# Expert masks that read exponentials from SBUF and compare them with the exponential of a threshold

## The reference

```python
s1 = einsum('bshd,nd->bshn', q1, K1)            # 8 heads, 32 keys each
s2 = einsum('bshd,nd->bshn', q2, K2)
v1, i1 = top_k(s1, 10);  v2, i2 = top_k(s2, 10)
all_scores = (v1[..., :, None] + v2[..., None, :]).reshape(..., 100)
vals, best = top_k(all_scores, 10)              # the 10 best pairs of a head
scores = softmax(vals)
h = gelu(x . w_down[expert]) * scores
out = einsum('bshk,bshkd->bsd', h, w_up[expert])
```

## Time and profile before

| | |
|---|---|
| median of 3 runs | 1143.75 us (1143.23 to 1144.29) |
| the profiled execution's own time | 1142.8 us |
| its span in the trace | 1141.0 us |
| mean granted TensorE clock | 0.97 (1.00 in the steady rounds) |
| busy: PE, ACT, DVE, POOL | 1015.9, 960.2, 880.9, 824.6 us |
| share of the span | 89%, 84%, 77%, 72% |
| one steady round | 32.42 us |

### The profile page before, as it was taken

How to read it: one execution, slowest core, us unless ns; L and a number is a source line. 1 busy time by engine, 2 the same in 40 slices (tenths; PEclk the granted TensorE clock), 3 DMA queues, 4 the chain that set the end, 5 groups by cost and what they waited for, 6 DMA issues and landing times.

```text
span 1141.0 us, 34446 instructions
## 1 busy us (share of the span) xinstructions
PE 1015.9 (89%) x11656; PEld 769.5 (67%) x11656; DVE 880.9 (77%) x2929; ACT 960.2 (84%) x2252; POOL 824.6 (72%) x871
## 2 busy tenths in 40 slices
PE   3588999999999999999999999999999999999755
PEld 2466777766677777766776777667777776677433
DVE  1427788888888888888888888888888888888763
ACT  1558899999999989999999999999899899998652
POOL 0234777887777777987777778877777788777755
PEclk9899899999999999999999999999999999999875
DMA  5000000000000000000000000000000000000000
GB/s 142 24 13 14 4 14 16 16 14 16 16 12 8 16 16 16 16 14 16 16 4 16 16 16 16 14 16 16 5 15 16 16 16 14 14 13 7 4 3 5
DMA packets 36683, 18.78 MB, mean 16 GB/s; under 512 B 13632, under 2 KB 36256, under 8 KB 36512
## 3 DMA queue, kind: packets, MB, share of 16 engines
q1 hardware_dynamic: 36512, 16.58, 5.4%
HBM read 14.47 MB, written 2.10 MB: 15 GB/s over the span
## 4 chain that ended last, share of the span: by engine, by line
POOL 35%; DVE 21%; issue 14%; ACT 14%; PE 14%; SPq 1%; DMA 1%; POOLq 1%; DVEq 0%; ACTq 0%
POOL wsum L1038 23%; ACT p L649 7%; POOL feat L1022 5%; DVE cand L908 5%; DVE mw L937 4%; DVE best L913 3%; DVE best L903 3%; PE psXT L330 3%; ACT ew L737 3%; PE psXT L414 3%; POOL rstd L976 3%; ACT am L686 2%; PE psF L533 2%; POOL cand L1007 2%; SPq L230 1%
## 5 line engine op out<-in xcount | busy, mean ns | idle before, releaser
L1038 POOL TENSOR_TENSOR wsum<-wsum,mw 128x1024 f32<-128x1024 f32 x192 | 451.8, 2353 | 165.6 <-DVE mw L937 160.0
L937 DVE SCALAR_TENSOR_TENSOR mw<-psF,cut,ew 128x1024 f32<-128x1024 f32 x256 | 326.1, 1281 | 61.9 <-ACT ew L737 58.6
L737 ACT ACTIVATE ew<-psF,lnz 128x1024 f32<-128x1024 f32 x256 | 288.3, 1127 | 14.5 <-PE psF L533 11.3
L649 ACT ACTIVATE p<-psXT,negmax 128x128 f32<-128x128 f32 x512 | 182.2, 387 | 2.6 <-DVE negmax L810 2.5
L533 PE MATMUL psF<-sel,usT 128*128 128x512 f16 x512 | 158.6, 393 | 24.7 <-DVE mw L937 21.8
L330 PE MATMUL psXT<-cT,q 96*128 96x128 f32 x1024 | 141.0, 281 | 22.9 <-ACT p L649 18.5
L330 PEld LDWEIGHTS psXT<-cT,q 96*128 96x128 f32 x1024 | 129.1, 195 | 43.5 <-ACT p L649 35.3
L989 POOL TENSOR_TENSOR p<-p,rrow 128x512 f32<-128x512 f32 x128 | 131.5, 1038 | 16.9 <-DVE rrow L819 16.8
L365 PE MATMUL psXT<-pT,c 128*96 128x512 f32 x256 | 135.4, 612 | 0.0
L380 PE MATMUL psXT<-vo,uT 96*128 96x128 f32 x1024 | 121.2, 277 | 0.0
L649 ACT ACTIVATION_READ_ACCUMULATOR p<-psXT,negmax 128x1 f32 x512 | 117.2, 229 | 0.0
(11 more groups left out here) (137 smaller groups left out, 2266.1 us busy)
## 6 DMA issues: line engine op xcount, KB each, us to landing
cT<-cT_dram SPq DMA_DIRECT2D x32, 96.0 KB, 2.0
c<-c_dram SPq DMA_DIRECT2D x32, 96.0 KB, 2.1
x<-x_dram SPq DMA_DIRECT2D x32, 64.0 KB, 2.1
xr<-x_dram SPq DMA_DIRECT2D x32, 64.0 KB, 1.8
y_dram<-y SPq DMA_DIRECT2D x32, 64.0 KB, 2.1
wqT<-wqT_dram SPq DMA_DIRECT2D x1, 512.0 KB, 4.1
wo<-wo_dram SPq DMA_DIRECT2D x1, 512.0 KB
wdT<-wdT_dram SPq DMA_DIRECT2D x1, 512.0 KB
```

Of the source, the lines that this page charges most:

```text
L649: ins = act.activation(p[:, k, i, :], bank[BANK[f"x.s{k}"]][:, i * M:i * M + M], ACT.Exp, bias=negmax[:, k, i:i + 1], accum_out=rowsum[:, ...
L737: done(f"e.x{h}", act.activation(ew[:, h % NEW, :], bank[BANK[f"e.s{h}"]], ACT.Exp, bias=lnz[:, t % 4, h:h + 1]))
L937: done(f"e.w{h}", dve.scalar_tensor_tensor(out=mw[:, h % NMW, :], in0=bank[BANK[f"e.s{h}"]], scalar=cut[:, t % 4, h:h + 1], in1=ew[:, h % ...
L1038: done(f"e.a{h}", pool.tensor_tensor(wsum[:, t % 2, :], mw[:, 0, :] if h == 1 else wsum[:, t % 2, :], mw[:, h % NMW, :], ALU.add))
```

## The change

The mask no longer reads the sums in PSUM. Since the exponential grows with its argument, a sum is over the threshold where its exponential is over that of the threshold; so `e.w{h}` takes `ew` in SBUF both as the number compared and as the number kept, and compares with `ecut`, the exponential of the threshold plus `lnz`. `k.cand` now leaves the plain sum of the 10th and 11th (`cutsum`); a new step `k.cutl` on VectorE halves it and adds `lnz`, and a new step `k.ecut` on ScalarE takes the exponential. The steps of TensorE that waited until a mask had read a bank wait for ScalarE's read (`e.x{h}`) in its place. The orders gain the two steps and are otherwise as before.

```diff
@@ TensorE: every wait on e.w{h} for a bank is now one on e.x{h}; the core of it
             def hidden(t):
-                after(pe, "e.w5", t - 1)
+                after(pe, "e.x5", t - 1)
...
                     if h == 0:
-                        pe.wait_ge(s["e.w2"], t + 1)
+                        pe.wait_ge(s["e.x2"], t + 1)
...
                     elif h == 2:
-                        after(pe, "e.w6", t - 1)
+                        after(pe, "e.x6", t - 1)
                         at_ends(pe, "e.gelu", t)
                     elif h == 3:
-                        pe.wait_ge(s["e.w1"], t + 1)
+                        pe.wait_ge(s["e.x1"], t + 1)
...
@@ ScalarE
+            def cut_exp(t):
+                act.wait_ge(s["k.cutl"], t + 1)
+                after(act, "e.w7", t - 4)
+                done("k.ecut", act.activation(ecut[:, t % 4, :], cutl[:], ACT.Exp))
+            steps["k.ecut"] = cut_exp
@@ VectorE
                 dve.wait_ge(s["k.inner"], t + 1)
                 after(dve, "k.eb", t - 1)
-                after(dve, "e.w7", t - 4)
...
-                lc.link(dve.tensor_tensor(cut[:, t % 4, :], best[:, :, TOPK], best[:, :, TOPK + 1], ALU.add))
-                lc.wait()
-                done("k.cand", dve.tensor_scalar_mul(cut[:, t % 4, :], cut[:, t % 4, :], 0.5))
+                done("k.cand", dve.tensor_tensor(cutsum[:, t % 2, :], best[:, :, TOPK], best[:, :, TOPK + 1], ALU.add))
...
+            def cut_shifted(t):
+
+                dve.wait_ge(s["k.lnz"], t + 1)
+                dve.wait_ge(s["k.cand"], t + 1)
+                after(dve, "k.ecut", t - 1)
+                done("k.cutl", dve.scalar_tensor_tensor(out=cutl[:], in0=cutsum[:, t % 2, :], scalar=0.5,
+                                                        in1=lnz[:, t % 4, :], op0=ALU.mult, op1=ALU.add))
+            steps["k.cutl"] = cut_shifted
...
                     dve.wait_ge(s[f"e.x{h}"], t + 1)
+                    dve.wait_ge(s["k.ecut"], t + 1)
...
-                    done(f"e.w{h}", dve.scalar_tensor_tensor(out=mw[:, h % NMW, :], in0=bank[BANK[f"e.s{h}"]],
-                                                             scalar=cut[:, t % 4, h:h + 1], in1=ew[:, h % NEW, :],
+                    done(f"e.w{h}", dve.scalar_tensor_tensor(out=mw[:, h % NMW, :], in0=ew[:, h % NEW, :],
+                                                             scalar=ecut[:, t % 4, h:h + 1], in1=ew[:, h % NEW, :],
                                                              op0=ALU.is_ge, op1=ALU.mult))
```

More of the change, by code:

```diff
@@ L105, in build @@
         best = sb("best", [128, FH, 16])
-        cut = sb("cut", [128, 4, FH])
+        cutsum = sb("cutsum", [128, 2, FH])
+        cutl = sb("cutl", [128, FH])
+        ecut = sb("ecut", [128, 4, FH])
         ebest = sb("ebest", [128, FH, TOPK])
@@ L506, in step @@
                     if h == 0:
-                        pe.wait_ge(s["e.w2"], t + 1)
+                        pe.wait_ge(s["e.x2"], t + 1)
                     elif h == 1:
                         after(pe, "e.add", t - 2)
-                        at_ends(pe, "e.w7", t - 1)
+                        at_ends(pe, "e.x7", t - 1)
                         at_ends(pe, "e.add", t - 3)
@@ L516, in step @@
                     elif h == 2:
-                        after(pe, "e.w6", t - 1)
+                        after(pe, "e.x6", t - 1)
                         at_ends(pe, "e.gelu", t)
                     elif h == 3:
-                        pe.wait_ge(s["e.w1"], t + 1)
+                        pe.wait_ge(s["e.x1"], t + 1)
                     elif h == 4:
-                        pe.wait_ge(s["e.w3"], t + 1)
+                        pe.wait_ge(s["e.x3"], t + 1)
                     elif h == 5:
                         after(pe, "e.gate", t - 1)
-                        at_ends(pe, "e.w0", t)
+                        at_ends(pe, "e.x0", t)
                     elif h == 6:
                         after(pe, "e.gelu", t + 1)
-                        at_ends(pe, "e.w5", t)
+                        at_ends(pe, "e.x5", t)
                     elif h == 7:
-                        pe.wait_ge(s["e.w4"], t + 1)
+                        pe.wait_ge(s["e.x4"], t + 1)
                     pe.wait_ge(s["k.ksb"], t + 1)
@@ L540, in w_turn @@
             def w_turn(t):
-                after(pe, "e.w0", t + 1)
-                at_ends(pe, "e.w6", t)
+                after(pe, "e.x0", t + 1)
+                at_ends(pe, "e.x6", t)
                 pe.wait_ge(s[f"e.a{FH - 1}"], t + 1)
@@ L550, in experts_out @@
             def experts_out(t):
-                after(pe, "e.w7", t + 1)
+                after(pe, "e.x7", t + 1)
                 at_ends(pe, "e.add", t - 1)
@@ L775, in _ @@
             ltop, lsp, lc, lz = (Chain(dve, own[n], k) for n, k in
-                                 (("dve_top", 16), ("dve_split", 1), ("dve_cand", 4), ("dve_zsum", 1)))
+                                 (("dve_top", 16), ("dve_split", 1), ("dve_cand", 3), ("dve_zsum", 1)))
             stat_chain = {n: Chain(dve, sem("dve_" + n.replace(".", "_")), k)
@@ L1060 @@
     "x.w0": 2, "e.x6": 5, "t.norm": 3, "x.w2": 2, "t.sb": 3, "k.eb": 4, "t.v": 3, "k.lnz": 4, "t.pexp": 3,
-    "e.x2": 4, "x.e2": 2,
+    "e.x2": 4, "k.ecut": 4, "x.e2": 2,
 }
@@ L1066 @@
     4, "k.top": 4, "x.low": 2, "k.split": 4, "e.w7": 5, "y.res": 3, "k.cand": 4, "e.w6": 5, "k.z": 4, "e.add":
-    6, "x.x2": 2, "t.path": 3,
+    6, "x.x2": 2, "k.cutl": 4, "t.path": 3,
 }
```

## The result

The changed kernel takes 1415.89 us, median of 4 runs (1412.7 to 1417.54), where the kernel before took 1143.49 in the same comparison: ratio 1.2374, 95% interval 1.2343 to 1.2405. That is 272 us more, a steady round of 41.2 us in place of 32.4. Forecast were 1445 us and 42.1. Times in this document are medians of the runs in the usual state of the chip, which leaves out one slower run each of masks_all (1705.82 us, granted clock 0.558) and masks_not03 (1345.1 us); with them the medians are 1370.0 and 1328.08 us, the numbers that later expectations use.

What follows compares the result with a forecast made beforehand. The prediction took a loop of GpSimd's queue (26.3 us), then VectorE's candidates and a mask (6.1 us), as the bound. Masks 8.7 + `k.cutl` stall 1.2 - threshold 0.2 = 9.7 us a tile, times 31 = 301: 1445 us, range 1195 to 1485.

Steps and rivals of the forecast that it cites:

- The loop and its lack of cover: GpSimd from `e.a6` to `k.inner`, then VectorE's candidates and a mask; slower GpSimd has at most 0.41 us cover per tile.
- One engine stops the other, in both orders: VectorE masks beside GpSimd: whichever instruction starts first blocks the other engine's for its whole length; chance 0.45.
- the bounds: Cost of a mask beside GpSimd: below, nothing; above, one engine's instruction stops the other's for its whole length.
- half price: Rival: masks and GpSimd share by turns, half a mask's length reaches GpSimd, 4.4 us a tile, 1279 us; chance 0.22.
- VectorE alone: Rival: GpSimd never gives way, only masks wait, 2 us a tile on the path, 1205 us; chance 0.13.
- No contention: Rival: masks and GpSimd don't disturb each other, the change is a little faster, 1141 us; chance 0.20.
- Seven masks at 1.25, 8.7 a round: Seven of eight masks in GpSimd's full stretch each stop GpSimd once for 1.25 us, 8.7 us a round.
- The stall at `t.path`: On VectorE, `k.cutl` waits for `e.a6` to end and delays `t.path`, so GpSimd starts `t.feat` later: +1.2 us a tile.
- The threshold's -0.2: Second threshold instruction removed on VectorE, so the mask ahead of `e.a6` starts earlier: -0.2 us a tile.
- The earlier banks: PSUM banks freed one mask earlier for TensorE: taken as 0, at most -22 us in all.
- The clock: TensorE, with 11 us idle a round, may fall below granted clock 1.00, adding to the forecast; no size given.
- the upper end: Full blocking between VectorE's two-input SBUF instructions and GpSimd: 9.7 us a tile, 1445 us; chance 0.45.

Runs made afterwards that it cites:

- masks_all: The kernel before with all eight masks reading `ew` in SBUF for both inputs, compared with `cut`, bank waits and threshold untouched: 1366.69 us, ratio 1.1957.
- masks_not03: The kernel before with six masks reading `ew` in SBUF for both inputs, heads 0 and 3 still on PSUM: 1319.67 us, ratio 1.1587.
- mask_6: The kernel before with only head 6's mask reading `ew` in SBUF for both inputs: 1145.1 us, ratio 1.0009.
- masks_21: The kernel before with only the masks of heads 2 and 1 reading `ew` in SBUF for both inputs: 1258.74 us, ratio 1.1008.
- after_one_input: The changed kernel with each mask a `tensor_scalar` that reads `ew` once, the product with the weight left out: 1276.1 us, ratio 1.1141.
- thr_only: The kernel before with only the steps `k.cutl` and `k.ecut` added; masks wait for `k.ecut` but still compare with `cut`: 1194.05 us, ratio 1.0431.
- double_sel: The kernel before with doubled sums in PSUM, the second threshold instruction left out and ScalarE's exponential scaled by one half: 1138.98 us, ratio 0.9938.
- after_warm: The changed kernel with 12 idle products of 128x512 on TensorE ahead of `t.fturn`: 1408.28 us, ratio 1.2295.
- after_warm2: The changed kernel with 8 idle products on TensorE ahead of `t.fturn` and `e.s1`'s products made six times: 1412.66 us, ratio 1.2346.
- masks_457: The kernel before with only the masks of heads 4, 5 and 7 reading `ew` in SBUF for both inputs: 1234.97 us, ratio 1.0802.
- masks_03: The kernel before with only the masks of heads 0 and 3 reading `ew` in SBUF for both inputs: 1201.04 us, ratio 1.0508.

## Why the prediction was right, and where its sum was off

**The loop and its lack of cover: right.** The change lengthened GpSimd's stretch, and the wait ahead of `e.a6` stayed at 5.00 us, as the earlier trace rows had 5.05. Counted from the candidates' sum, where before has 584.97: `t.path`'s user starts at 4.96 us (before 4.03), `k.root` at 24.77 (17.95).

**One engine stops the other, in both orders: shown.** Neither end of the bounds was in the trace of before; mask_6, masks_21 and the rows above settle on the upper one. This is also what the Trainium skill, SBUF — State Buffer, section Who interferes with whom, says; the trace agrees, in both orders (root 0.55 to 1.57 behind a mask; mask 1.28 to 2.26 behind an addition). Who gives way it does not show in every case: the first instruction of `t.feat` began 0.52 us ahead of the masks and waited. The prediction told that section's rule on a single SBUF input without its exception, a one-input form at double rate; the exception agrees too (norm 1.03 to 1.49 in after_one_input). The rivals of half price and of VectorE alone fell: single instructions of 0.55 us lose 1.0 while the mask beside them keeps its 1.28, and both engines lose. No contention fell with 223 us.

**Seven masks at 1.25, 8.7 a round: the term that was sized too high.** In the round of the changed kernel shown above the masks cost 7.9. An instruction held up once is 1.0 us longer, not 1.25: `e.a7` +0.97, a norm +1.00, two roots +1.02 and +0.97. `t.feat` beside two masks is 2.84 longer. The seventh mask, at 732.01, lengthens nothing of GpSimd; `x.r{k}` comes late behind it and GpSimd waits 1.31 us for that. Less 0.23 for a shorter wait ahead of `k.root`, this makes 7.9. The groups alone, at full clock, cost less: heads 2 and 1 2.2 us a round, 0 and 3 1.8, 4, 5 and 7 2.7, together 6.7. What the masks add to one another in company is read from the rows, not shown by a run of its own.

**`k.cutl`: right.** The stall at `t.path` is 1.1 us. The prediction's 1.2 is a rounding of its own sum: 588.84 + 0.17 + 0.93 is 589.94, 1.10 behind 588.84. thr_only lost 1.6 a round because of its rounds with time at half clock; at full clock they lost 1.1. The gap was not filled there to prove it.

**The threshold's -0.2: right.** `e.a6` starts 1.54 us after the candidates' sum, before 1.71; alone it is worth some 5 to 7 us (double_sel: 0.17 in a steady round, 7.1 by the medians).

**The earlier banks: no sign of a gain,** as taken. It was not tried by itself.

**The clock: named as a risk, not counted.** It costs 46 us in masks_21. In the changed kernel it stands at 0.50 for 10.3 us of the round:

```profile
722.30:732.60 10.30, 8.19 (x64) 5.54 (x67) 5.48 (x7) 5.38 (x17) 9.99 (x8) 0.50 0.01 2
...
715.78:757.02 41.24, 33.97 (x364) 25.79 (x364) 30.36 (x91) 30.48 (x71) 32.54 (x27) 0.88 0.04 11
```

and yet it costs nothing there that shows in a round: rounds of after_warm at full clock take the same 41.2 us, and the whole time fell by only 3 (after_warm2) to 9 us (after_warm) by the ratios. That GpSimd and VectorE in turn are a path of equal length (`k.root` at 24.7 us in all three kernels) is read from their traces, not shown by a run of its own.

In all, 7.9 for the masks + 1.1 - 0.2 = 8.8 a round, as measured, where 9.7 was forecast. The loop and the turn-taking were foreseen; the forecast lay 29 us too high because each mask was counted with its whole length. That the upper end was the true one was a choice at 0.45, which no trace of before could decide.

## What to carry to other kernels

Before an operand moves from PSUM to SBUF, look at what GpSimd does at that moment. Here a VectorE instruction with two SBUF inputs and GpSimd took turns, and so did a one-input `tensor_scalar` of 0.75 us; even one of 128x8 numbers waited 1.3 us. Check it at the one place where they don't meet before reading an average. And a loss can have a second price: where TensorE waits longer in a round, it may come back at half clock. Whether that costs anything depends on which path is the longer by then (46 us in masks_21, nothing in a round of the changed kernel), so compare rounds of the same trace at either clock, fill the gap and measure.

## What the runs showed of the hardware

- An instruction of GpSimd held up by a 1.28 us mask is 1.0 us longer; by one of 0.75 us, 0.46 us (norm) and 0.23 to 0.45 us (roots). The wait shows in the row's duration, not as idle time.
- The row that starts first is not always the one that goes first: an instruction of GpSimd that began 0.52 us ahead of two masks in a row took 3.09 us in place of 0.24.
- The mask takes 1284 ns with its first input in PSUM or in SBUF alike; a `tensor_scalar` on the same 128x1024 numbers in SBUF with a pointer scalar, 0.75 us.
- Gaps of 2.56 us on TensorE were followed by half clock for 3.4 to 6.8 us, gaps of 3.02 and 2.11 us in one round (the changed kernel) by half clock for 10.3 us. The length of a gap alone did not tell: 1.04 us (masks_457) and 2.0 us (thr_only) were followed by 3.4 us of half clock in some rounds and by none in others, 1.09 us in masks_03 by none.
